# Three banks in turn for value products and row maxima, in an attention block on one core

## The reference

```python
q = jnp.einsum('btc,hcd->bhtd', xs, Wq)   # k and v likewise
scores = jnp.einsum('bhtd,bhsd->bhts', q, k) * scale
att = jax.nn.softmax(scores, axis=-1)
out = jnp.einsum('bhts,bhsd->bhtd', att, v)
out = jnp.transpose(out, (0, 2, 1, 3)).reshape(B, T, -1)
out = out @ Wproj + bproj
x = x + out   # reshaped; q, k, v are made of the normalised x
```

## Time and profile before

| | us |
|---|---|
| median of 3 runs | 4950.16 (4949.59 to 4951.74) |
| the profiled execution: span from the first to the last instruction | 4946.9 |
| PE busy | 4705.1 |
| ACT busy | 2886.6 |
| DVE busy | 2775.5 |
| POOL busy | 2326.6 |

### The profile page before, as it was taken

One profiled execution on the slowest core, in us unless ns is written; L12 is line 12 of the kernel. 1 busy time (PEld: TensorE's weight loads), 2 busy tenths in 40 slices (PEclk: granted clock), 3 DMA queues, 4 the chain that ended last, 5 costly groups with the idle time before them and its releaser, 6 DMA issues.

```text
span 4946.9 us, 73065 instructions
## 1 busy us (share of the span) xinstructions
PE 4705.1 (95%) x20608; PEld 3505.4 (71%) x20608; DVE 2775.5 (56%) x5284; ACT 2886.6 (58%) x5507; POOL 2326.6 (47%) x1837
## 2 busy tenths in 40 slices
PE   7999999999999999999999999999999999999998
PEld 5777767777676776767767677676776767767675
DVE  5655646556465564655646556465564655646454
ACT  4665646556465564655646566464664646656465
POOL 2444545445454454544545445454444545445455
PEclk9999999999999999999999999999999999999999
DMA  2111111111111111111111111211112111111101
GB/s 69 34 37 55 31 53 35 46 46 32 52 34 50 43 34 54 31 53 41 32 54 35 51 41 30 63 28 53 37 30 62 35 49 35 32 61 34 53 23 51
DMA packets 156934, 212.71 MB, mean 43 GB/s; under 512 B 56544, under 2 KB 57568, under 8 KB 156512
## 3 DMA queue, kind: packets, MB, share of 16 engines
q1 hardware_dynamic: 156512, 207.47, 15.0%
HBM read 105.12 MB, written 34.08 MB: 28 GB/s over the span
## 4 chain that ended last, share of the span: by engine, by line
issue 50%; POOL 42%; PE 6%; POOLq 1%; ACT 1%; DVE 0%; DMA 0%; SPq 0%; ACTq 0%; DVEq 0%
POOL prob_l L1031 32%; POOL o L1048 6%; POOL res L1054 3%; PE bank L517 1%; PE bank L561 1%; POOLq L1030 1%; POOL rstd L1023 1%; PE bank L578 1%; PE bank L690 1%; PE bank L692 1%; PE bank L691 1%; PE bank L571 0%; PE bank L572 0%; POOLq L1047 0%; DMA xs<-in_x 0%
## 5 line engine op out<-in xcount | busy, mean ns | idle before, releaser
L1031 POOL TENSOR_TENSOR prob_l<-prob,prob_h 128x512 fp32r<-128x512 f32 x1408 | 1803.5, 1288 | 2470.5 <-ACT prob_h L710 2452.6
L710 ACT ACTIVATE prob<-bank 128x512 f32<-128x512 f32 x2048 | 1237.6, 604 | 1698.6 <-PE bank L572 1579.3
L864 DVE TENSOR_REDUCE smax<-bank 128x1 f32<-128x512 f32 x2048 | 1349.1, 684 | 1012.6 <-PE bank L578 997.8
L710 ACT ACTIVATE prob_h<-bank 128x512 fp32r<-128x512 f32 x2048 | 1236.7, 604 | 198.6 <-PE bank L692 154.9
L690 PE MATMUL bank<-prob_h,vh 128*128 128x512 f32 x2048 | 832.6, 407 | 117.9 <-ACT acc L781 99.3
L578 PE MATMUL bank<-k_hl,q_hh 128*128 128x512 f32 x2048 | 802.5, 436 | 33.6 <-DVE smax L864 30.4
L571 PE MATMUL bank<-q_hh,k_hl 128*128 128x512 f32 x2048 | 824.0, 402 | 0.5 <-ACT prob_h L710 0.5
L572 PE MATMUL bank<-q_lm,k_h 65*128 65x512 f32 x2048 | 813.8, 397 | 0.0
L692 PE MATMUL bank<-prob_l,vh 128*128 128x512 f32 x2048 | 809.6, 395 | 0.0
L691 PE MATMUL bank<-prob_h,vl 128*128 128x512 f32 x2048 | 809.0, 395 | 0.0
L803 DVE TENSOR_TENSOR prob_l<-prob,prob_h 128x512 fp32r<-128x512 f32 x640 | 508.0, 804 | 511.9 <-ACT prob_h L710 511.8
(11 more groups left out here) (58 smaller groups left out, 4393.2 us busy)
## 6 DMA issues: line engine op xcount, KB each, us to landing
xs<-in_x SPq DMA_DIRECT2D x128, 256.0 KB, 2.8
q_hh<-q_hh SPq DMA_DIRECT2D x256, 128.0 KB, 2.2
k_hl<-k_h SPq DMA_DIRECT2D x256, 128.0 KB, 2.4
inv_b<-inv_dram SPq DMA_DIRECT2D x256, 128.0 KB, 2.8
res<-in_x SPq DMA_DIRECT2D x128, 256.0 KB, 2.7
out_x<-res SPq DMA_DIRECT2D x128, 256.0 KB, 2.0
q_lm<-q_lm SPq DMA_DIRECT2D x256, 2.0 KB
den<-acc SPq DMA_DIRECT2D x256, 2.0 KB, 1.7
```

The costliest lines, as they stand in the source:

```text
L710: return nc.scalar.activation(out, ps[ST + bank][:, :], ACT.Exp, scale=SCALE)
L864: nc.vector.tensor_reduce(smax[:, j:j + 1], ps[SM + j % 2][:, :], AX.X, ALU.max).then_inc(rows_used, 1)
L1031: nc.gpsimd.tensor_tensor(prob_l[:, r3, :], prob[:, ring2, :], prob_h[:, r3, :].bitcast(F32), ALU.subtract).then_inc(prob_l_pool, 1)
```

## The change

- The three banks 3 to 5 take turns. `VALUE_BANK` says which one holds the value product of each half of each head; the row matmuls use the other two, by age. The function `turns` plays through a step and gives for each row matmul and each first value product the last user of its bank: a row of this step, a value half, or none in this step. `turn_free` turns that into the wait. For none it waits for all 16 maxima that the step before issued.
- The first value product of a half no longer waits for the copy of the half before but for the last user of its own bank. For `tc` = 0 that is none in this step, in every head; for `tc` = 1 it is a row between 0 and 6 of this step.
- The other work and the row matmuls of the blocks 0 and 8 go behind the value product.
- `mt` becomes `nc.tensor.transpose`, which needs one pass where the matmul needs two.
- The numbers of maxima per block, the entries and their blocks are the same as before, and so is the order on ACT, DVE, POOL and SP.

```diff
-ST, SM, PVB, WB = 0, 3, 5, 6
+ST, TURN, WB = 0, 3, 6
+VALUE_BANK = (0, 1, 2, 0, 1, 2, 0, 1, 2, 0, 1, 2, 0, 1, 2, 1)
-    "plain": ((0, 8), (), (0, 7, 14)),
+    "plain": ((), (), (0, 7, 14)),
...
+def turns(h, per_slot):
+    user = [None, None, None]
+    row_turn, value_turn = [], []
+    age = {b: -1 for b in range(3)}
+    user[VALUE_BANK[2 * h - 1]] = ("value", -1)
+    for i in range(BLOCKS):
+        tc, t = divmod(i, 8)
+        value, after = VALUE_BANK[2 * h + tc], VALUE_BANK[(2 * h + tc + 1) % BLOCKS]
+        if t == 0:
+            value_turn.append(user[value])
+            user[value] = ("value", tc)
+            if tc:
+                age[VALUE_BANK[2 * h]] = 2 * i
+        for n in range(per_slot[i], 0, -1):
+            late = t == 7 and n == 1
+            bank = min((b for b in range(3) if b != value and not (late and b == after)),
+                       key=lambda b: (t != 7 or b != after, age[b]))
+            row_turn.append((bank, user[bank]))
+            user[bank] = ("row", len(row_turn) - 1)
+            age[bank] = 2 * i + 3 - n
+    return row_turn, value_turn
...
+        def turn_free(eng, s, user):
+            if user is None:
+                eng.wait_ge(rows_used, s.heads(BLOCKS, 1))
+            elif user[0] == "row":
+                eng.wait_ge(rows_used, s.heads(BLOCKS, 1, user[1] + 1))
+            elif not (s.section == "first" and user[1] < 0):
+                eng.wait_ge(acc_ready, s.heads(2, 0, user[1] + 1))
...
-                    nc.tensor.matmul(w[0:4, 0:P], nmax[:, a * 4:(a + 1) * 4], ident[:, :],
-                                     start=True, stop=True).then_inc(mt_done, 1)
+                    nc.tensor.transpose(w[0:4, 0:P], nmax[:, a * 4:(a + 1) * 4], ident[:, :]).then_inc(mt_done, 1)
...
-                    pe.wait_ge(rows_used, s.heads(BLOCKS, 1, j - 1))
-                    row_scores((s.k + 1) % 2, j)
+                    bank, user = s.row_turn[j]
+                    turn_free(pe, s, user)
+                    row_scores((s.k + 1) % 2, j, bank)
...
-                    if t == 0 and not (first and tc == 0):
-                        pe.wait_ge(acc_ready, s.heads(2, 0, tc))
+                    if t == 0:
+                        turn_free(pe, s, s.value_turn[tc])
...
-                    bank = PVB
+                    bank = TURN + VALUE_BANK[2 * s.h + tc]
...
                     if i not in s.first[0]:
                         other_work(s, i)
+                    other_rows(s, i)
```

More of the change, by code:

```diff
@@ L94 @@
 FIRST = {
-    "plain": ((0, 8), (), (0, 7, 14)),
-    "values": ((0, 8), (), ()),
-    "norm": ((0, 8), (), ()),
-    "tokens": ((0, 8), (15,), (8,)),
-    "next": ((0, 8), (), (6, 13, 14)),
-    "proj": ((0, 8), (), ()),
+    "plain": ((), (), (0, 7, 14)),
+    "values": ((), (), ()),
+    "norm": ((), (), ()),
+    "tokens": ((), (15,), (8,)),
+    "next": ((), (), (6, 13, 14)),
+    "proj": ((), (), ()),
 }
@@ L190, in __init__ @@
         self.looped = section == "body"
+        self.row_turn, self.value_turn = turns(
+            self.h, max_blocks(self.h, self.has_next, self.looped and k == 8))
     def at(self, per_batch, const):
@@ L573, in scores, with row_scores @@
                                  start=False, stop=True).then_inc(scores_ready, 1)
-            def row_scores(slot, j):
+            def row_scores(slot, j, turn):
                 t, half = divmod(j, 2)
-                nc.tensor.matmul(ps[SM + j % 2][:, :], q_hh[:, slot, t * P:(t + 1) * P],
+                nc.tensor.matmul(ps[TURN + turn][:, :], q_hh[:, slot, t * P:(t + 1) * P],
                                  k_hl[:, slot, half * 512:(half + 1) * 512], start=True, stop=True).then_inc(rows_ready, 1)
@@ L613, in _ @@
                     pe.wait_ge(rows_used, j - 1)
-                row_scores(0, j)
+                row_scores(0, j, j % 2)
                 if j == 9:
@@ L644, in other_work, with other_rows @@
                     entry(kind, a, lo, hi, bk, before, (s.h + (2 if kind == "qn" else 1)) % NH, wait)
+            def other_rows(s, i):
                 per_slot = max_blocks(s.h, s.has_next, s.section == "body" and s.k == 8)
@@ L780, in copy_out @@
                     act.wait_ge(o_ready, s.heads(2, 0, tc - 1))
-                nc.scalar.copy(acc[:, tc, :], ps[PVB][:, :]).then_inc(acc_ready, 1)
+                nc.scalar.copy(acc[:, tc, :], ps[TURN + VALUE_BANK[2 * s.h + tc]][:, :]).then_inc(acc_ready, 1)
             def take_in_step(s, kind, a):
@@ L860, in take, with take_max @@
                     last.then_inc(taken[bank], 1)
-            def take_max(j, count):
+            def take_max(j, count, turn):
                 dve.wait_ge(rows_ready, count)
-                nc.vector.tensor_reduce(smax[:, j:j + 1], ps[SM + j % 2][:, :], AX.X, ALU.max).then_inc(rows_used, 1)
+                nc.vector.tensor_reduce(smax[:, j:j + 1], ps[TURN + turn][:, :], AX.X, ALU.max).then_inc(rows_used, 1)
             def combine(half, used):
@@ L908, in _ @@
                     for j in range(10, BLOCKS):
-                        take_max(j, j + 1)
+                        take_max(j, j + 1, j % 2)
                     combine(1, BLOCKS)
@@ L944, in maxima @@
                         for _ in range(per_slot[i - 1] if i else 0):
-                            take_max(hj, s.heads(BLOCKS, 1, hj + 1))
+                            take_max(hj, s.heads(BLOCKS, 1, hj + 1), s.row_turn[hj][0])
                             hj += 1
```

## The result

| | before | after |
|---|---|---|
| median, us | 4950.95 (4949.59 to 4955.44, 4 runs) | 5083.07 (5078.06 to 5088.30, 4 runs) |
| ratio | | 1.0267 [1.0252, 1.0281] |
| span of the profiled execution | 4946.9 | 5076.3 |
| mean granted clock of TensorE | 0.994 | 0.975 |

What follows compares the result with a forecast made beforehand. PE, busy 95% of the span, was taken as the bound. Per batch 6.8 + 0.9 - 1.4 = +6.3 us, +97 in all, gave about 5047 from 4946.9; clock falls (+96) made it 5143, range 5030 to 5175.

Steps and rivals of the forecast that it cites:

- waits, blocks 0 and 8 and what follows: First value products wait for maxima instead of the copy: +6.8 us per batch at block 0, +0.9 at block 8.
- clock: PE's clock falls behind seven longer waits per batch, 4.7 falls instead of 0.7, 1.5 us each: +96 us, bounds 0 and +150.
- transpose: mt in one pass saves 0.11 us in 13 of 16 entries per batch: -1.4 us per batch, bounds 0 and -2.8.
- The wait at block 0: Value product waits for the last maximum: +1.54 three times, +0.80 twice, +0.56; +6.8 us per batch, bounds 6.0 to 7.2.
- Block 8: Product waits for one of rows 0 to 6; 2.57 us stall in proj, net +1.5; sum over steps +0.9 us per batch.
- the stall's own give-back: Proj: part of block 8's 2.57 us stall comes back in block 10, where the projection entry waits for DVE; net +1.5.
- moves a block ahead and is paid once: Tokens: block 7's row waits for row 5, as row 7 does now in block 8; counted 0, bounds -0.5 to +0.6.
- the product that starts sooner at block 8: Block 8, no wait for the copy: 0.3 us of stall goes in each of two values steps; plain steps 0.
- two signs that I named: PEclk below 1.00 behind block 0 of values, norm, plain and tokens; wrong if the clock stays up behind waits over 2 us.
- the one that the clock stays up: Rival: maxima late at block 0, but no new clock falls; 5047 us, 5020 to 5070; chance 0.30.
- the copy was the real holder: Rival: at block 0 the maxima are in time and the stalls return; 4806 us, or 4863; chance 0.06.
- the new stalls are paid back downstream: Rival: slack on PE behind block 0 takes the new stalls back, so nothing much changes; chance 0.03.

Runs made afterwards that it cites:

- e6_busy_all: Changed kernel with the scores of block 0 (in proj also block 8) made four times ahead of the seven long waits: 4997.71 us, ratio 1.0101.
- e2_fixed_banks: Changed kernel with the banks and waits of before; work of blocks 0 and 8 stays behind the value product, mt one-pass: 4859.84 us, ratio 0.9813.
- e1_mt_only: Kernel before with only mt made a one-pass transpose; banks, order and waits as before: 4859.93 us, ratio 0.9814.
- e7_fixed_banks_late_wait: e1_mt_only with the first value product of a step also waiting for all 16 maxima of the step before: 5059.69 us, ratio 1.0226.
- e4_rows_by_13: Changed kernel with the row matmuls of block 14 in plain, values and norm moved to block 13 (norm: 12 and 13): 4897.95 us, ratio 0.9882.
- e3_busy_norm0: Changed kernel with the scores made four times instead of once only in block 0 of norm: 5076.71 us, ratio 1.0268.
- e8_rows_early_all: e4_rows_by_13 with the copy wait put back in block 8 of norm and one row instead of two in block 7 of proj: 4798.89 us, ratio 0.9706.

## Why the prediction was right, and where its terms were off

| term, us in all | predicted | measured | from |
|---|---|---|---|
| waits, blocks 0 and 8 and what follows | +120 | +138 | `e6_busy_all` less `e2_fixed_banks` |
| clock | +96 | +85 | after less `e6_busy_all` |
| transpose | -23 | -91 | `e1_mt_only` |
| sum | +193 | +132 | |

The kernels of the first and the third row stand in different sets, whose kernel before differs by 6 us, so each of the first two terms is good to about 6 us. `e6_busy_all` keeps a little of the clock's loss (0.994) and adds work to the waits, so the cut between the two is the one that this experiment makes. Falls of the clock also hide in the rows of waits and of the transpose, since they differ from kernel to kernel behind the same wait. Priced at the prediction's 1.5 us each, an estimate, they leave -79 for the transpose (8 falls fewer than before), about -20 for the moved work (`e2_fixed_banks` has 13 falls more than `e1_mt_only` in the same time) and about +145 for the waits (15 falls at proj go, 10 in norm and tokens come). The prediction's first term holds the moved work too, so it stands at +120 against some +125, and the clock at +96 against some +86.

- *The wait at block 0*: right, by size and place. The stalls of 2.54, 2.54, 2.07, 2.16, 2.16 and 2.49 forecast are 2.55, 2.55, 2.04, 2.16, 2.15 and 2.50, and `e6_busy_all` has the additions 1.54, 1.54, 1.54, 0.80, 0.80 and 0.56 one by one. `e7_fixed_banks_late_wait` shows that the wait is the cause, and `e4_rows_by_13` that it is late rows that make it.
- *Block 8*: the stall in proj is right, 2.57 as forecast, but the net is right only by luck. Its block 8 is 2.75 longer than before and its block 10 1.04 shorter: +1.7, forecast +1.5. I took block 10 for the stall's own give-back. `e2_fixed_banks` has the same 1.04 without the stall, from the moved work alone, and against it after has 2.5 us more in block 8 and nothing back in block 10: the stall is paid in full. In tokens the stall that I said "moves a block ahead and is paid once" is +1.82 in block 7 and -0.87 and -0.43 behind it: +0.5, inside the bound.
- *Not foreseen*: block 9 of norm. I had put 0 or a small gain on the product that starts sooner at block 8; it shifts POOL's low part in front of a small DVE operation, and costs 1.4 us of waiting per batch, 20 us in all, and a second fall of the clock in every norm step. The trace of before had the evidence, an operation of 4 columns that takes 1.27 us (2639.32) beside POOL's.
- *The transpose*: the term that failed, -23 against -91, of which some 79 are its own. The share that arrives was right (13 of 16 entries, at 0.38 us, are 79 over the kernel), the price of one was not. I priced a pass at 0.11 us, from transposes that stand behind one another; "the loading of the weights and the waits ahead of it stay" was wrong. An entry costs 0.64 with float32 operands and 0.26 as a transpose. The idle time of the loads, 90.5 us of issue ahead of line 557, stood in the groups by line of before, but I had read only the line of the matmuls there, whose idle time was 2.7.
- *The clock*: that it falls behind such waits is right; that the size came out near is in part luck, by a rate that did not hold. I spread the falls evenly, 10 of 15 behind every long wait, 70 in all. In after 28 of the 105 waits have one: 15 of 15 in norm, 1 of 15 in the second values step, for the same 2.55 us, and at proj 10 of 15, as before, though the wait there grew from 1.93 to 2.50. What made up for the missing ones is that the norm falls are about twice as dear (at 0.55 over 7 us, 12 matmuls or 2.8 us, against the 1.5 taken) and that 20 more stand at places I did not have. So two signs that I named did not go my way: the clock is not below 1.00 behind block 0 of the values, plain and tokens steps but for a single batch or none, and it stayed at its upper level behind 77 of 105 waits over 2 us. `e3_busy_norm0` and `e7_fixed_banks_late_wait` show that the place is no property of the step, and the proj step, with 10, 2 and 15 falls of 15 in before, `e1_mt_only` and `e2_fixed_banks` behind a wait of 1.93 us, that it is no property of the wait's length either. What decides which of several long waits is followed by a fall stays open; only the total is tested.
- *The rivals*: the one that the clock stays up is out by the clock of 0.975 and by `e6_busy_all`. Its 5047 lies near the result only by the transpose: with 68 us less for that and 18 more for waits it is 4997, the time of `e6_busy_all`, and after is 85 above. That the copy was the real holder is out too: the releaser after is the maxima. That the new stalls are paid back downstream is out by `e7_fixed_banks_late_wait`, where the wait at block 0 alone costs 200 us.

The Trainium skill, "TensorE: Matmul & The Clock Gate", section "HAM oscillation — how this bites in real kernels", ties such falls to idle gaps longer than any of the waits in this loop. The windows after disagree, with 0.55 behind a stall of 2.55 us.

## What to carry to other kernels

When a wait is swapped for another, look up in the trace when the new releaser ends, not only that the old one is the last today: here the row maxima ended up to 1.5 us after the copy, and issuing the last rows of three kinds of step a block or two sooner turned a loss of 2.7% into a gain of 1.2%, the same in proj with one small wait put back into 2.9%. Of this gain 1.9% is the transpose alone, and the banks in turn are worth the last 1.1. Price a small matmul by the distance from the matmul before it to the one behind it, its weight load included, and not by its records. If an idle gap of PE of 2 us or more can't be removed, filling it with matmuls that are thrown away can pay (85 us on the kernel after; 0.1 to 0.3% on `e8_rows_early_all`, hardly clear of noise), but fill all such gaps: with one filled, the falls of the clock came up in the next. And look at the clock in both kernels before an experiment's gain is put down to its edit.

## What the runs showed of the hardware that I had not expected

- A float32 matmul of 4 by 128 that stands alone among others costs 0.64 us of PE's time, as a transpose 0.26: the load of its weights starts 0.32 us after the matmul ahead of it instead of together with it.
- The same stall of 1.93 us at one place was followed by a fall of the clock in 10, 2 and 15 of 15 batches in three kernels that differ elsewhere. The same stall of 2.55 us is followed by a fall of the clock in 15 of 15 batches in one place and in 1 of 15 in another, and a fall taken away in one place comes up again in the next (norm -2.79 us per batch, plain +2.58).
- A DVE operation on 128x4 numbers took 0.17 us, or 1.21 when POOL's 128x512 operation had started 0.07 before it.
